# First expert layer: rows of a tile brought by two transposing transfers and one transfer of the carried columns

## The reference, cut to what matters

```
t = t + _L0_ffn_ref(_ln_t(t), W_router, W1, b1, W2, b2)

def _L0_ffn_ref(x, W_router, W1, b1, W2, b2):
    probs = softmax(x_flat @ W_router)                  # 8 experts
    topk_p, topk_i = top_k(probs, 2);  topk_p /= topk_p.sum()
    combine = (one_hot(topk_i, E) * topk_p[..., None]).sum(axis=1)
    for e in range(E):
        h = relu(x_flat @ W1[e] + b1[e])                # 128 -> 512
        y = h @ W2[e] + b2[e]                           # 512 -> 128
        out = out + combine[:, e:e + 1] * y
```

## Time and profile before

| what | value |
|---|---|
| time, median of 3 runs | 1365.71 us (1361.33 to 1366.5) |
| the profiled execution's own time | 1350.42 us |
| its span, first to last instruction | 1348.5 us |
| mean granted PE clock | 0.914 |
| busy: PE / PEld / DVE / ACT / POOL | 81% / 54% / 68% / 58% / 41% |
| `phase_experts0`, SP's first issue to the next phase's first | 437.24 to 894.57 us |

### The profile page before, as it was taken

The page is one execution under the profiler, slowest core; times in us unless marked ns, Lnnn a source line. Parts: engine busy times, 40 slices in busy tenths (PEclk is TensorE's granted clock), DMA queues, the critical chain, the costliest instruction groups (busy, mean ns, idle before and its releaser), DMA issues. The chain is left out here.

```text
span 1348.5 us, 34743 instructions
## 1 busy us (share of the span) xinstructions
PE 1087.7 (81%) x9956; PEld 732.4 (54%) x9957; DVE 914.9 (68%) x2139; ACT 782.6 (58%) x2044; POOL 548.0 (41%) x401
## 2 busy tenths in 40 slices
PE   6869796876520999999999999948999999946586
PEld 2324353433310999999999999923444434413354
DVE  3653355554445777777778878726999999975586
ACT  5855486765540676566666766726665665613364
POOL 0000025635573233233333333334999999990000
PEclk9989898988855999999999999979999999975599
DMA  6100001341112111111111111121022221102000
GB/s 199 60 1 0 1 12 37 112 139 54 32 63 69 48 44 41 40 41 43 40 42 41 45 41 43 42 83 32 16 63 62 62 62 51 40 20 79 1 1 32
DMA packets 60527, 65.25 MB, mean 48 GB/s; under 512 B 9841, under 2 KB 50301, under 8 KB 60336
## 3 DMA queue, kind: packets, MB, share of 16 engines
q1 hardware_dynamic: 49616, 46.47, 11.9%
q0 software_dynamic: 8832, 17.00, 3.8%
q10 hardware_dynamic: 2016, 0.94, 0.3%
HBM read 37.12 MB, written 28.55 MB: 49 GB/s over the span
## 5 line engine op out<-in xcount | busy, mean ns | idle before, releaser
L933 ACT ACTIVATE m_hh<-ps 128x256 f16<-128x256 f32 x584 | 216.9, 383 | 130.0 <-PE ps L890 72.6
L970 DVE SCALAR_TENSOR_TENSOR m_hl<-ps,m_hh 128x256 f16<-128x256 f32 x584 | 242.8, 422 | 69.4 <-ACT m_hh L933 57.0
L833 POOL DMA_INDIRECT expert_out<-m_result,m_token x148 | 144.5, 976 | 326.7 <-DVE m_result L989 321.3
L870 PE MATMUL ps<-m_x,weights 128*128 128x128 f16 x1168 | 213.4, 220 | 4.8 <-DVE m_hl L970 3.6
L874 PE MATMUL ps<-m_x,weights 128*128 128x128 f16 x1168 | 212.8, 220 | 0.1
L871 PE MATMUL ps<-m_x,weights 128*128 128x128 f16 x1168 | 212.8, 220 | 0.0
L776 POOL DMA_INDIRECT dispatched<-d_rows,slot x128 | 130.1, 1016 | 202.7 <-DVE slot L684 107.7
L888 PE MATMUL ps<-weights,m_hh 128*128 128x128 f16 x1160 | 209.5, 219 | 2.2
L890 PE MATMUL ps<-weights,m_hl 128*128 128x128 f16 x1160 | 209.2, 219 | 0.0
L889 PE MATMUL ps<-weights,m_hh 128*128 128x128 f16 x1160 | 209.2, 219 | 0.0
L1098 POOL TENSOR_TENSOR iv_pool_sum<-iv_pool_sum,iv_pool_part 128x1024 f32<-128x1024 f32 x80 | 188.7, 2359 | 11.7 <-DVE iv_pool_part L1313 3.8
(11 more groups left out here) (307 smaller groups left out, 2302.7 us busy)
## 6 DMA issues: line engine op xcount, KB each, us to landing
m_rows<-dispatched SPq DMA_DIRECT2D x152, 65.5 KB
X<-x SPq DMA_DIRECT2D x16, 512.0 KB, 4.5
iv_got<-expert_out SPq DMA_DIRECT2D x16, 512.0 KB, 4.2
out<-X SPq DMA_DIRECT2D x16, 512.0 KB, 3.1
Y<-w_moe SPq DMA_DIRECT2D x8, 512.0 KB
expert_out<-m_result,m_token POOLq DMA_INDIRECT x148
dispatched<-d_rows,slot POOLq DMA_INDIRECT x128
Y<-w_last SPq DMA_DIRECT2D x1, 2048.0 KB
```

What stands on the lines that cost most here:

```text
L833: pool.indirect_dma_start(env.yt, bass.IndirectOffsetOnAxis(ap=token[:, k:k + 1], axis=0), result[:, k, :], None, bounds_check=TOKENS - 1, ...
L870: pe.matmul(out, high, xh, start=True, stop=False)
L933: act.activation(hh[e][:, part_cols[h]], hidden[e][h], ACT.Relu).then_inc(hi_ready[e], 1)
L970: dve.scalar_tensor_tensor(hl[e][:, cols], hidden[e][h], 0.0, hh[e][:, cols], ALU.max, ALU.subtract).then_inc(h_split[e], 1)
```

## The change

A row's float16 numbers 127 and 255 are no longer written from the data: POOL fills them once with 1 and 0 at the start of `phase_tokens0`, and ACT (L570) and DVE (L623) write 127 columns where they wrote 128. In `phase_experts0` SP issues three transfers for each tile in place of one: two transposing ones, 128 rows by 128 float16 each, which land in `x` channel by partition, and one of the three carried columns. `x` has eight places (the ring) in place of one. PE's turning products, ACT's and DVE's `take`, the identity in float16 and the filling of the last partition are gone. `up` waits for `rows_ready` itself.

```diff
 # phase_tokens0
+            pool.memset(halves[:, :, C - 1], 1.0).then_inc(filled, 1)
+            pool.wait_ge(filled, 1)
+            pool.memset(halves[:, :, 2 * C - 1], 0.0).then_inc(filled, 1)
+            pool.wait_ge(filled, 2)
-                act.activation(by_bank(rows_of(n)[:, :, 0:C]), tiles_of(n)[:, :, :, 0:C], ACT.Copy).then_inc(normed, 1)
+                act.activation(by_bank(rows_of(n)[:, :, 0:C - 1]), tiles_of(n)[:, :, :, 0:C - 1], ACT.Copy).then_inc(normed, 1)
-                dve.tensor_tensor(by_bank(at[:, :, C:2 * C]), tiles_of(n)[:, :, :, 0:C], by_bank(at[:, :, 0:C]), ALU.subtract)\
+                dve.tensor_tensor(by_bank(at[:, :, C:2 * C - 1]), tiles_of(n)[:, :, :, 0:C - 1], by_bank(at[:, :, 0:C - 1]), ALU.subtract)\
 # phase_experts0
-        rows = sb("m0_rows", [P, RING, ROW])
-        idh = sb("m0_idh", [P, P], F16)
-        x = sb("m0_x", [P, 2, P], F16)
-        xh, xl = x[:, 0, :], x[:, 1, :]
+        x, tails = sb("m0_x", [P, RING, 2, P], F16), sb("m0_tails", [P, RING, CARRIED])
-        turn = [env.psum[3][:, k * HALF:k * HALF + P] for k in range(2)]
-        gate = lambda i, g: rows[:, at(i), C + g:C + g + 1].rearrange("p k c -> p (k c)")
+        gate = lambda i, g: tails[:, at(i), g:g + 1].rearrange("p k c -> p (k c)")
 # SP
-                    sp.wait_ge(landed[k % (RING // 2)], j * 32 + (16 if k < RING // 2 else 32))
+                    sp.wait_ge(landed[k % (RING // 2)], j * 96 + (48 if k < RING // 2 else 96))
                     sp.sem_inc(rows_ready, 1)
...
                     sp.wait_ge(out_ready, i + 1)
-                    sp.dma_start(rows[:, k, :], env.xg[bass.ds(row, SLOT), :]).then_inc(landed[k % (RING // 2)], 16)
+                    for part_ in range(2):
+                        sp.dma_start_transpose(x[:, k, part_, :], env.xg16[bass.ds(row, SLOT), part_ * C:(part_ + 1) * C])\
+                            .then_inc(landed[k % (RING // 2)], 16)
+                    sp.dma_start(tails[:, k, :], env.xg[bass.ds(row, SLOT), C:ROW]).then_inc(landed[k % (RING // 2)], 16)
 # PE
-            def turn_rows(i):
...
-                pe.wait_ge(x_ready, i + 2)
+                if e == 0:
+                    pe.wait_ge(rows_ready, i + 1)
+                xh, xl = (x[:, at(i), part_, :].rearrange("p k s -> p (k s)") for part_ in range(2))
...
-                    if m == 0:
-                        pe.wait_ge(xl_ready, i + 2)
...
                 down(i, 0, pair[0])
-                turn_rows(i + 2)
                 up(i + 1, 1, following[1])
...
-            turn_rows(0)
...
-            turn_rows(1)
 # ACT and DVE, each
-            def take(i):
...
-            take(0)
...
-            take(1)
...
-                take(i + 2)
```

More of the change, by code:

```diff
@@ L390, in phase_tokens0 @@
             ("rows_ready", "sq_ready", "ln_ready", "rstd_ready", "scaled"))
+        filled = sem("t0_filled")
         normed, taken, steps = sem("t0_normed"), sem("t0_taken"), sem("t0_steps")
@@ L789, in phase_experts0 @@
         landed = [sem(f"m0_landed{k}") for k in range(RING // 2)]
-        rows_ready, turned, x_ready, xl_ready = sem("m0_rows_ready"), sem("m0_turned"), sem("m0_x_ready"), sem("m0_xl_ready")
+        rows_ready = sem("m0_rows_ready")
         h_ready, hi_ready, h_split, y_ready = ([sem(f"m0_{n}{e}") for e in range(2)] for n in ("h_ready", "hi_ready", "h_split", "y_ready"))
         part_ready, out_ready, result_free = (sem(f"m0_{n}") for n in ("part_ready", "out_ready", "result_free"))
-        stored, ready = [sem(f"m0_stored{k}") for k in range(OUTS)], sem("m0_ready")
-        rows = sb("m0_rows", [P, RING, ROW])
-        halves = rows[:, :, :].rearrange("p k c -> p (k c)").bitcast(F16).rearrange("p (k c) -> p k c", k=RING)
-        idh = sb("m0_idh", [P, P], F16)
-        x = sb("m0_x", [P, 2, P], F16)
-        xh, xl = x[:, 0, :], x[:, 1, :]
+        stored = [sem(f"m0_stored{k}") for k in range(OUTS)]
+        x, tails = sb("m0_x", [P, RING, 2, P], F16), sb("m0_tails", [P, RING, CARRIED])
         hh, hl = ([sb(f"m0_{n}{e}", [P, H0], F16) for e in range(2)] for n in ("hh", "hl"))
@@ L897, in tile @@
                 down(i, 0, pair[0])
-                turn_rows(i + 2)
                 up(i + 1, 1, following[1])
                 down(i, 1, pair[1])
-            pe.wait_ge(ready, 3)
             pe.sem_inc(part_ready, 1)
-            turn_rows(0)
             for e in range(2):
                 up(0, e, PAIR_LIST[0][e])
-            turn_rows(1)
             for p in range(PAIRS):
@@ L933, in high @@
                     act.activation(hh[e][:, part_cols[h]], hidden[e][h], ACT.Relu).then_inc(hi_ready[e], 1)
-            act.wait_ge(ready, 3)
-            act.sem_inc(x_ready, 1)
-            take(0)
             high(0, 0)
             high(0, 1)
-            take(1)
             total = count(act, 0, PAIRS, MAX_TILES)
@@ L951, in _ @@
         def _(dve):
-            dve.tensor_copy(idh[:, :], env.idf[:, :]).then_inc(ready, 1)
-            dve.memset(x[96:P, 0, :], 1.0).then_inc(ready, 1)
-            dve.memset(x[96:P, 1, :], 0.0).then_inc(ready, 1)
             for e in range(2):
@@ L957, in _ @@
             dve.sem_inc(out_ready, RING)
[L958 to L965, removed]
             def low(i, e, h):
@@ L1732, in build @@
         env.xg, env.yt = xg, yt
+        env.xg16 = xg.bitcast(F16)
         setup_constants(nc, env, a)
```

## The result

The changed kernel takes 1546.9 us (median of 4 runs, 1543.3 to 1552.5) against 1365.3 us before: ratio 1.136, 95% interval 1.132 to 1.139. The forecast was 1528, with 1438 to 1600 as its range. In the medians that is 181.5 us more, where 162 were forecast; in the two profiled executions the span grew from 1348.5 to 1550.7 us.

The account below looks back on a forecast made before the run. PE was taken to bound the kernel before; with the change SP's issues become the bound at 4.08 us per tile against PE's 2.91, lengthening the phase by 162 us: 1365.7 plus 162 gives 1528 us, range 1438 to 1600.

Parts of the forecast that it names:

- PE bounds the kernel, and SP has 198 us of slack: Experts' phase before: PE busy 429.3 of 435.5 us sets the pace; SP waits 198.0 us for free ring places.
- Two of the signs: Signs expected in the experts' phase: PE's busy share about two thirds, and the next phase starting near 1057 us.
- x, the hold of one transposing issue, 1.2 us: SP's queue, experts' phase: time one transposing issue holds SP, taken as 1.2 us, the middle of 0.97 and 1.37.
- The step from tile to tile, 3.87 us: SP, experts' phase: 1.27 us as before plus two transposing issues with steps, 2 x (1.2 + 0.1), per tile.
- The spare tiles stand at the end: End of experts' phase: SP issues 152 tiles where PE needs 146; the six spare ones now stand on the path.
- The data movement is hidden: DMA engines, experts' phase: 384 rows per tile instead of 128 take 0.8 us of a 4 us tile, hidden.
- The dispatch costs nothing: Dispatch before the experts: POOL's two fills and the shorter ACT and DVE writes were taken to cost 0.
- Rival A: Experts' phase: a transposing issue holds SP only 0.33 us, PE stays the bound and sheds 16 us; 1350 us, chance 0.12.
- Rival B: Experts' phase: SP is held until the data has landed, 1.94 us per transposing issue; +387, 1753 us, chance 0.03.
- Rival C: Experts' phase: PE, idling, falls to 1.2 GHz for good and is the bound again; +362 us, 1728 us, chance 0.01.

Follow-up runs that it names:

- e2: The changed kernel with one transposing transfer of 256 columns per tile in place of two of 128; 1362.5 us, ratio 1.009 against the kernel before.
- e1: The changed kernel with plain copies in place of the two transposing transfers, rows left unturned (another result); 1335.4 us, ratio 0.987 against the kernel before.
- e4: The kernel before with only the dispatch edits: POOL's two fills, and ACT and DVE writing 508 numbers instead of 512; 1356.7 us, ratio 1.001.
- e5: The changed kernel with one transposing transfer of 256 columns per tile and each group's last tile announced later; 1339.9 us, ratio 0.992 against the kernel before.
- e3: The changed kernel, both transposing transfers kept, each group's last tile announced after the next group's first issues; 1519.0 us, ratio 1.123 against the kernel before.

## Why the prediction was right, point by point

*PE bounds the kernel, and SP has 198 us of slack.* Right. The slack is gone and PE waits for SP. Two of the signs came out weaker than I had them: PE's busy share fell to 75% and not to two thirds, and the next phase began at 1095.2 us and not near 1057.

*x, the hold of one transposing issue, 1.2 us.* It was chosen between POOL's indirect issue (0.97) and SP's longest (1.37), and it measured 1.12 in the median. The means over 152 tiles, taken from the trace's own durations, are 1.11 for the first of a tile and 1.18 for the second, 2.29 together where the sum had 2.4. This term decided the sign, and it was an argued choice; nothing in the trace of before proved it, and the 1.37 above it was the hold of a plain issue. That it came so close is in part luck: e2 speaks against the reason that I gave for it (the transfer is built piece by piece), since twice the columns add only 0.07 us. A fixed price of the instruction is what the runs show, and what it consists of is open.

*The step from tile to tile, 3.87 us.* It measured 4.05 within a group: 0.11 us less for the two holds, 0.10 more for the small issue (0.43 where I kept 0.33), 0.15 more for the steps between issues (0.14 and 0.20, where I had 0.1 each, without a row), and 0.04 more of bookkeeping. This is the mis-sized term: the small parts around the hold, not the hold. With the 1.76 us at a group's end (I had 1.7) a group took 7 x 4.05 + 5.80 = 34.1 us, not 32.7, and 19 groups make the 28 us by which the phase grew more than forecast.

*The spare tiles stand at the end.* Right in kind: the block waited for SP, 5 us beyond what POOL needed; I had about 2.

*The data movement is hidden.* Shown by e1, and by e2 for transposed data. SP's queue between 460 and 1060 us in the changed kernel, and between 500 and 850 us in e1:

```profile
q1 hardware_dynamic: 65419, 9.50, 10.4%
```

```profile
q1 hardware_dynamic: 52725, 8.21, 14.5%
```

In the changed kernel that is 463 packets for a tile where I had 384, but each takes 0.104 x 600 x 16 / 65,419 = 15 ns where I had 32. Together it is 0.44 us of each DMA engine's time per tile, half of my 0.8.

*The dispatch costs nothing.* Shown by e4. The two fills took 0.3 us each, and ACT's write of 508 numbers took 602 ns where 512 had taken 598.

*Rival A*, the short hold, gave 1350 us, 16 less than before. The premise was false, but its sum is what e1 measured once the premise was made true, 14.7 us. It put the turn of the sign at x = 0.66, where a group takes 8 x (1.27 + 2 x 0.76) + 1.7 = 24.0 us. e2 and e5 lie on either side of that: 8 x 3.07 = 24.6 us and a phase 10.2 us longer than before, 8 x 2.91 = 23.3 us and one 14.2 us shorter. And e5, just at the 23.2 us from which SP was to count at all, has PE's whole gain. The sentence of the Trainium skill behind it ("Advanced Engine Details and Errata", "X-Bar Transpose (TRN2)", transposing as fast as regular) can hold for the data and does not hold for the issue. A packet of SP's queue took 15 ns here and 0.145 x 350 x 16 / 52,725 = 15 ns in e1 with plain copies, while the issue took 1.12 us in place of 0.33. The Trainium skill's other page, "VectorE: DVE Perf Modes" ("The three transpose paths"), with its 1309 ns for one transpose by DMA, came nearer, though it doesn't say that the issuing sequencer is held, and its figure lies 0.19 us above the median here.

*Rival B*, a hold as long as the landing, 1.94 us: refuted by the median of 1.12, and by 1546.9 us where it had 1753.

*Rival C*, the clock: it fell for a short time at nearly each group's end, and the cost was hidden. There PE stands for 3.4 to 4.2 us, and then the granted clock falls. The timeline row that ends one such gap in the changed kernel, and the windows around it:

```profile
523.67 0.23 PE L866 MATMUL ps<-m_x,weights 128*128 x1 [3.75 <-SPq L816]
```

```profile
520.00:524.00 4.00, 0.33 (x5) 0.29 (x6) 1.32 (x4) 0.40 (x2) 1.59 (x2) 1.00 0.18 39
524.00:528.00 4.00, 4.00 (x50) 4.00 (x49) 1.06 (x3) 1.45 (x4) 0.00 (x0) 0.64 0.15 28
528.00:532.00 4.00, 3.54 (x59) 3.37 (x57) 2.42 (x7) 1.93 (x6) 0.98 (x1) 0.94 0.12 17
```

In the second one PE works through at a mean clock of 0.64, the lower level (1.2 GHz) for part of it, with 50 products in 4 us where the full clock has 72. In the trace 18 gaps are this long, and 17 of them are followed by such a spell, of 25 to 56 products some 0.107 us apart; the one at 1001 us is not. A spell costs PE 1.3 to 2.9 us. Behind the 72 gaps of 1.0 to 2.0 us in this kernel none is seen. PE had 1.05 us of waiting in each tile to catch up in, and the phase went by SP's steps. e3 bears that out: most spells went with the long gaps, and the phase fell by SP's waits and no more. Right in the forecast: the clock comes back, and the slack hides it.

The long gap is not the only occasion, though. In e3, whose gaps reach 2.4 us, 6 of the 11 over 2.0 us are followed by a spell; one of them, and the window behind it:

```profile
668.66 0.23 PE L872 MATMUL ps<-m_x,weights 128*128 x1 [2.03 <-SPq L815]
```

```profile
670.00:673.00 3.00, 3.00 (x31) 3.00 (x29) 0.86 (x3) 1.34 (x4) 0.57 (x1) 0.50 0.20 44
```

And e1 has one of 31 products though no two products start more than 0.74 us apart once the phase runs; e2 has one of 23, behind three gaps of 0.7 to 0.9 us:

```profile
780.00:782.00 2.00, 2.00 (x21) 2.00 (x20) 0.93 (x3) 0.48 (x2) 0.49 (x1) 0.50 0.24 41
```

So what makes the clock fall stays open; what the traces show is that it does so seldom behind short gaps and behind 17 of the 18 of 3.4 us and more.

## What to carry to other kernels

An issue counts by the time for which it holds its queue, and that is another price than the transfer's own. Before work goes from a busy engine to transfers, set the queue's slack (its wait for free places, 198 us here) against what the new issues add, their holds and the steps to them (152 x 2.6 us), and for the hold of an instruction that the trace lacks take the nearest rows from both sides and work out the value at which the sign turns (0.61 to 0.66 us here). When such a change fails, count instructions before bytes: one issue for both halves, and one wait moved behind the next group's first issues, turned 13.6% slower into 0.8% faster. The gain is small, and it was measured on another chip than the loss, each against the kernel before on its own.

## What the runs showed of the hardware that I had not expected

- A transposing issue from SP of 128 rows holds the queue 1.12 us for 128 columns of float16 and 1.19 us for 256 (medians of 304 and 152), and it does so with no other row transfer on its way too.
- A plain issue behind a transposing one holds SP longer: the same transfer of 12 bytes by 128 rows took 0.43 us in the median in the changed kernel and 0.41 in e2 and e5, and 0.33 behind plain ones in e1.
- A gap of 1.1 us in front of PE left the products at 0.055 us behind the first few; a gap of 3.4 to 4.2 us was followed in 17 of 18 cases by 25 to 56 products at half the pace, and a window of such a place shows a granted clock of 0.64 for 4 us. Gaps of 2.1 to 2.4 us in e3 were followed by such a spell 6 times in 11, and e1 has one with no gap over 0.74 us.
